# First attention stage: TensorE issues its groups in another order within a turn, and ScalarE's last two copies change places

## The reference, cut to what matters

```python
x = x + L0_xattn(layernorm(x), ctx_1024, pos, pos, Wq, Wkv, Wout, bout)

q = (x @ Wq).reshape(b, n, 32, 8)
k, v = split(ctx @ Wkv)                 # 32 heads of 8
q = apply_axial_rope(q, pos_map)
k = apply_axial_rope(k, ctx_pos_map)
logits = einsum('bhqd,bkhd->bhqk', q, k) * scale
attn = einsum('bhqk,bkhd->bqhd', softmax(logits), v)
return attn.reshape(b, n, 256) @ Wout + bout
```

## Time and profile before

| what | us |
|---|---|
| median of three runs | 1014.71 |
| the profiled execution's own time | 1014.0 |
| span of its trace, first to last instruction | 1012.0 |
| TensorE busy in the span | 863.5 (85%) |
| VectorE, ScalarE, GpSimd busy | 674.9, 427.6, 334.1 |
| mean granted TensorE clock | 0.958 |

### The profile page before, as it was taken

The page is one execution under the profiler, slowest core; times in us unless marked ns, Lnnn a source line. Parts: engine busy times, 40 slices in busy tenths (PEclk is TensorE's granted clock), DMA queues, the critical chain, the costliest instruction groups (busy, mean ns, idle before and its releaser), DMA issues. The chain is left out here.

```text
span 1012.0 us, 25976 instructions
## 1 busy us (share of the span) xinstructions
PE 863.5 (85%) x9368; PEld 644.2 (64%) x9368; DVE 674.9 (67%) x1581; ACT 427.6 (42%) x1027; POOL 334.1 (33%) x292
## 2 busy tenths in 40 slices
PE   0799999999999899999979999999998860288883
PEld 0477777777777689898846666666665640155552
DVE  5577877777787675555467777777776489546652
ACT  1244434344443432332556666666666660022330
POOL 1444434334343031000033333333333110247763
PEclk9999999999999999999999999999999985589997
DMA  9300000000001000000001111111110199855542
GB/s 296 94 14 17 10 16 16 10 16 10 16 13 34 2 1 12 0 0 0 3 11 23 31 31 31 31 31 31 31 31 25 49 350 306 210 146 94 92 71 31
DMA packets 62074, 56.60 MB, mean 56 GB/s; under 512 B 24017, under 2 KB 57169, under 8 KB 62033
## 3 DMA queue, kind: packets, MB, share of 16 engines
q1 hardware_dynamic: 55888, 46.61, 15.8%
q0 software_dynamic: 6144, 9.44, 5.5%
HBM read 41.81 MB, written 14.22 MB: 55 GB/s over the span
## 5 line engine op out<-in xcount | busy, mean ns | idle before, releaser
L404 ACT ACTIVATE pr_t<-bank 128x512 f32<-128x512 f32 x128 | 76.4, 597 | 159.7 <-PE bank L300 158.9
L824 POOL TENSOR_TENSOR g_k_bd<-g_k_t,head_mask 128x1024 f32<-128x1024 f32 x32 | 60.6, 1893 | 134.4 <-ACT g_k_t L999 134.4
L312 PEld LDWEIGHTS bank<-v_bd,pr_t 128*64 128x64 f32 x2048 | 70.0, 137 | 26.5 <-issue 26.3
L300 PE MATMUL bank<-ident,sub 128*128 128x128 f32 x512 | 82.2, 283 | 3.6 <-ACT pr_t L404 2.9
L312 PE MATMUL bank<-v_bd,pr_t 128*64 128x18 f32 x2048 | 82.8, 214 | 0.1
L481 DVE TENSOR_TENSOR sub<-bank,top 128x2048 f32<-128x2048 f32 x32 | 73.3, 2292 | 3.9
L300 PEld LDWEIGHTS bank<-ident,sub 128*128 128x128 f32 x512 | 55.9, 141 | 30.8 <-issue 17.2
L261 POOL TENSOR_TENSOR rot<-part_a,part_b 128x512 f32<-128x512 f32 x32 | 40.7, 1273 | 103.4 <-DVE part_b L490 103.4
L477 DVE TENSOR_REDUCE top<-bank 128x32 f32<-128x2048 f32 x32 | 73.1, 2284 | 0.6 <-PE bank L288 0.4
L648 ACT ACTIVATE f_hid<-bank,b 128x128 f32<-128x128 f32 x128 | 36.5, 368 | 85.7 <-PE bank L594 85.7
L269 POOL TENSOR_TENSOR k_bd<-qk_t,head_mask 128x1024 f32<-128x1024 f32 x32 | 60.6, 1893 | 31.2 <-ACT qk_t L419 31.2
(11 more groups left out here) (203 smaller groups left out, 2001.5 us busy)
## 6 DMA issues: line engine op xcount, KB each, us to landing
e_w_gu<-in_experts_in SPq DMA_DIRECT2D x11, 768.0 KB, 10.7
table<-r_row SPq DMA_DIRECT2D x16, 320.0 KB, 8.6
e_w_d<-in_experts_out SPq DMA_DIRECT2D x11, 384.0 KB, 13.4
xres<-in_x SPq DMA_DIRECT2D x4, 1024.0 KB, 9.8
out<-xres SPq DMA_DIRECT2D x32, 128.0 KB, 1.7
xres<-in_experts_in SPq DMA_DIRECT2D x3, 768.0 KB, 19.8
keys_in<-in_ctx_t SPq DMA_DIRECT2D x32, 64.0 KB, 1.8
vals_in<-in_ctx_t SPq DMA_DIRECT2D x32, 64.0 KB, 1.8
```

The costliest lines, as they stand in the source:

```text
L300: m = pe.transpose(b_pr[:, j * P:(j + 1) * P], sub[:, v, cols], k.ident[:, :])
L312: m = pe.matmul(b_o[64 * b:64 * b + 64, hp * VW0:(hp + 1) * VW0], pr_t[:, e, j, b * S:(b + 1) * S], v_bd[:, v, b, hp, :], start=True, stop ...
L404: act.activation(pr_t[:, e, :, :].rearrange("p j q -> p (j q)"), b_pr[:, :], ACT.Exp).then_inc(a_exp, 1)
L824: pool.tensor_tensor(k_bd[:, v, :, :, :, :].rearrange("p c b h s -> p (c b) h s"), k_t[:, v, :, :].rearrange("p c (b a s) -> p (c b) a s", ...
```

## The change

On TensorE, within a turn: the transposes of `att` move from behind turned lot 3 to directly behind turned lot 2; the output product moves directly behind the key product; turned lot 3 moves behind the output product; values lots 1, 2 and 3 stand in a row at the end. No product is added or removed. The order is now: scores, turned lot 0, `xn`, `rot`, turned lot 1, values lot 0, value products, turned lot 2, `att`, query, key, output, turned lot 3, values lots 1, 2, 3. On ScalarE the copy of `att_t` moves ahead of exps(3). The waits go along with their groups.

```diff
                 if on[3]:
                     turn(w, v, 2)
-                    values(w, v, 1)
+                if on[4]:
+                    pe.wait_ge(a_att, f + 1)
+                    if on[0]:
+                        pe.wait_ge(a_xnTc, t + 1)
+                    if later(f, 1):
+                        pe.wait_ge(a_x1, f)
+                    for c in range(KC):
+                        m = pe.transpose(b_turn[:, c * P:(c + 1) * P], att[:, u, c * P:(c + 1) * P], k.ident[:, :])
+                    m.then_inc(a_attT, 1)
                 if on[0]:
                     pe.wait_ge(keys_done[u], 16 * (i + 1))
                     pe.wait_ge(a_xnTc, t + 1)
...
                     pe.matmul(b_qk[:, D:2 * D], keys_in[:, u, :], wk[:, :], start=True, stop=True).then_inc(a_qk, 1)
-                if on[3]:
-                    turn(w, v, 3)
-                if on[4]:
-                    pe.wait_ge(a_att, f + 1)
-                    if on[0]:
-                        pe.wait_ge(a_xnTc, t + 1)
-                    if later(f, 1):
-                        pe.wait_ge(a_x1, f)
-                    for c in range(KC):
-                        m = pe.transpose(b_turn[:, c * P:(c + 1) * P], att[:, u, c * P:(c + 1) * P], k.ident[:, :])
-                    m.then_inc(a_attT, 1)
-                if on[3]:
-                    values(w, v, 2)
                 if on[4]:
                     pe.wait_ge(a_attTc, f + 1)
                     for c in range(KC):
                         m = pe.matmul(b_turn[:, D:2 * D], att_t[:, u, c, :], wo[:, c, :], start=(c == 0), stop=(c == KC - 1))
                     m.then_inc(a_out, 1)
                 if on[3]:
+                    turn(w, v, 3)
+                    values(w, v, 1)
+                    values(w, v, 2)
                     values(w, v, 3).then_inc(a_pv, 1)
...
                 if on[3]:
                     exps(2)
-                    exps(3)
                 if on[4]:
                     act.wait_ge(a_attT, f + 1)
                     if later(f, 2):
                         act.wait_ge(a_out, f - 1)
                     act.activation(att_t[:, u, :, :].rearrange("p c q -> p (c q)"), b_turn[:, 0:D],
                                    ACT.Copy).then_inc(a_attTc, 1)
+                if on[3]:
+                    exps(3)
```

## The result

Ten runs of the changed kernel, in two sets beside runs of the kernel before on the same chip, gave:

| set | changed, median (range) | before, median | ratio, 95% interval |
|---|---|---|---|
| first, 4 runs | 999.64 us (996.73 to 1003.46) | 1015.44 us | 0.985 [0.981, 0.9891] |
| second, 6 runs | 1002.27 us (998.51 to 1009.43) | 1014.16 us | 0.9886 [0.9853, 0.9918] |

A forecast was written before the change was run, and what follows sets the result against it. TensorE's own sequence was taken to bound the kernel. Saving 0.46 us a turn over 28 turns, 12.9 us, less 0.15 us for fill and drain, took the median from 1014.7 to 1002.0 us, range 998.5 to 1006.5.

The forecast's parts named there:

- Turned lot 2, `att`: On TensorE, turned lot 2 stays at 4.04 us of the turn; the transposes of `att` follow at 4.54.
- The new wait for `v_bd`: Before TensorE's query product: it waits 0.24 us for both copies of `v_bd` and starts at 5.00 us.
- Warm output product: Output product directly behind the key product starts at the cheap price, taking 0.86 us instead of 1.06.
- rival of cold joins: Weight loads of moved groups are not hidden: output product 0.97 us, turned lot 3 0.58, total 1006.4; chance 0.12.
- Values lots in a row: At the turn's end, lots 1 and 2 cost 0.49 us each and lot 3 0.58 up to the scores.
- rival that lots in a row are dear: Each values lot following another costs 0.26 us more, so no change in time, 1016.5 us; chance 0.05.
- Cover of exps(3): Values lots 1 and 2 cover lot 3's wait for ScalarE's exps(3), ready at 8.55 us; cover 0.22 us.
- VectorE: VectorE has room: its wait for the key product shrinks from 0.88 to 0.68 us.
- Fill and drain: Outside the full turns: turn 3 counted 0, turns 32 and 33 each 0.07 us worse, together 0.15 us lost.
- The clock: Rival: thin work standing together lowers TensorE's granted clock, up to 1049 us if in every turn; chance 0.03.

The follow-up runs named there:

- e3: The changed kernel with values lot 1 put back behind turned lot 2; full turn 9.54 us, median 1006.77 us, ratio to before 0.9928.
- e2: The changed kernel with the transposes of `att` and the output product back behind turned lot 3, values lots still in a row; median 1034.88 us, ratio to before 1.0208.
- e4: The changed kernel with `rot` ahead of `xn`, value products ahead of values lot 0, and ScalarE's `qk_t` copy ahead of `xn_t`'s; 992.77 us, ratio to before 0.9788.
- e5: e4 with TensorE's wait for the `qk_t` copy put behind the two other waits ahead of the value products; 993.03 us, ratio to before 0.9779.
- e1: The kernel before with only ScalarE's copy of `att_t` moved ahead of exps(3); full turn 9.62 us, median 1012.07 us, ratio to before 0.9972.

## Why the prediction was right

It was right in sign and size, and in the steps that carry the gain:

- **Turned lot 2, `att`**: forecast at 4.04 and 4.54 us of the turn, measured 196.69 - 192.65 = 4.04 and 4.53.
- **The new wait for `v_bd`**: forecast, query product at 5.00, measured 5.00, and the price of resuming was 0.05 us as taken (197.60 to 197.65). The sign given for it, a wait on the copy's line, shows at the weight loads only.
- **Warm output product** (the step with no row of its own): 0.86 us forecast, 0.86 measured. The rival of cold joins, 0.12 of the chance, is out: key to output is 0.43, output to turned lot 0.86, turned lot 3 to values 0.53. Full-height loads hide behind full-height matmuls here: one load of the output product's weights takes 0.19 us (mean of L373, 190 ns), and yet its four matmuls stand 0.86 / 4 = 0.215 us apart; e3's warm query product shows it for yet another pair. The Trainium skill, page "TensorE: Matmul & The Clock Gate", section "Part 3: Packing small matmuls", states that loads overlap matmuls in flight only with a different row group, which this trace contradicts; but the same section also lets a load run ahead into a background weight buffer, and the trace agrees with that.
- **Values lots in a row**: forecast 0.49 + 0.49 + 0.58 = 1.56 us, measured 1.51 (201.95 - 200.44), so a lot behind a lot costs about 0.47. This accounts for the 0.03 to 0.05 us by which the turns are shorter than the forecast 9.35. The rival that lots in a row are dear is out with it.
- **Cover of exps(3)**: forecast ready at 8.55 of the turn. ScalarE's exponential ended at 200.55 + 0.60 = 201.15, 8.50 into the turn, 0.05 more is 8.55. Lot 3 started 0.2 us after that; e3 shows what happens without the cover.
- **VectorE**: the wait for the key product was to shrink from 0.88 to 0.68 us. The row of the changed kernel:

```profile
199.36 0.69 DVE L489 TENSOR_TENSOR part_a<-bank,cos_t 128x512 f32<-128x512 f32 x1 [0.68 <-PE bank L369]
```

- **Fill and drain**: turn 32 takes 322.69 - 313.78 = 8.91 us, 0.03 more than before where 0.07 was forecast, and the whole drain from its scores to the last output product 27.68 us against 27.60, 0.08 more where 0.15 was forecast. Turn 3 takes 9.44 us against 9.39, 0.05 more where 0 was forecast.
- **The clock** stayed at 1.00 between 60 and 300 us in every profile, that of e2 with its longer waits too. The rule of the same page, "Part 4: PE-mode transpose", that transposes do not count as activity, would have put the end of the turn at risk; nothing of that shows here, and these runs cannot test it alone, since scores follow at once.

The sum: the full turns took 274.65 - 261.00 = 13.65 us less, of which 0.2 is lost again ahead of them and in the drain, so 13.4, against 12.75 forecast. In the second profile of the changed kernel the same sum is 13.6: its full turns start at 52.57 instead of 52.78 us. The mis-sized term is the distance of values lots in a row, by 0.02 us each.

Two things in the prediction are not as it says. The transposes of `att` stood 7.04 - 4.54 = 2.50 us later before, not 2.3; nothing hangs on it. And the forecast's own range, 3.5 us either way, does not follow from the 2.8 and 1.5 us given for it, which add up to 4.3. That the second median lies within 0.3 us of the forecast is luck: the two medians of the same kernel are 2.6 us apart.

## What to carry to other kernels

When an engine is "busy" all the time, look at the distances from start to start of its groups: the same group at two prices is a join that can be moved. Put groups of one shape together, but only where a round trip through another engine stays covered: the same row of thin products gave 0.49 us a turn with the transposes of `att` moved early and cost 0.54 us a turn without. A reordering is worth calculating to the end: the wait that it creates (0.24 us here) was known from the rows before, and taking that one away as well gave another 0.30 us a turn, 8 us. Where one engine comes close behind another, compare a turn of the loop with the same turn written out ahead of it: a wait that only the loop has (0.75 against 0.58 us in e4) comes from how the loop is issued, not from the data.

## What the runs showed of the hardware that was not expected

- **The clock outside the full turns differs from execution to execution.** The same program, the changed kernel, has 0.53 between 36 and 44 us in its first profile and 0.79 in its second, like the kernel before; its experts' stage has 0.98 or 0.94 and takes 112 or 117 us. Around the last output product of the first attention e5 has 0.80 and e4 0.93 (320 to 345 us), and the kernel before (343 to 368), both profiles of the changed kernel (330 to 355) and e3 (334 to 359) have 1.00; whether that is the program or the execution is not shown. TensorE waits in between in these places, 0.97 us in the earlier trace rows. That goes with the scatter of up to 1% between runs, which a change of 1% has to be read against; the length of a full turn, the same to 0.01 us in both profiles of the changed kernel, resolves much more.
- **What it costs to resume after a wait depends on what the sequencer still has to do behind it.** TensorE resumed 0.05 us after ScalarE's copy at the query product of the changed kernel, where the trace has the wait on the first weight load itself. In e4's loop it took 0.23 us: the wait for the copy is an instruction of its own (L340), the register operation of the next wait (L342) stands behind it, and the loads come last. With the late wait last (e5) that register operation is gone from between them and 0.14 us remain in the even turns: the wait is still an instruction of its own there.
- **ScalarE shows the same.** Its copy of `att_t` started 0.39 us after the start of the last transpose in e1 and e2, the exponential 0.31 after that of its own. Both had idled before (1.96 us in e1, 1.66 in the earlier trace rows), so idling is not the cause. In e1 the trace has the copy's wait on a register operation at 202.87, and the copy at 202.95; the exponential carries its wait itself. The copy of `qk_t` in the even turns of e4 and e5 has such an operation ahead of it too, and starts 0.07 us later than in the odd ones. That these operations are the cause is read from where they stand in the traces; only TensorE's was moved by an experiment (e5).
